# Two layers of conditioned attention: projections and turns moved behind the products on row tiles in each key tile

## The chip, the cores and the metric

One core of one Trainium2 chip. The metric is the device time of one execution in microseconds (us); lower is better. The kernel before takes 514.0 us, the median of 3 runs (513.84 to 514.3).

## What is computed

Two layers on x of 4 batches, 512 tokens, 256 channels, with 16 heads of width 16. Cut to what matters:

```python
# layer 0
xm  = rmsnorm(x) * (1 + scale) + shift            # scale, shift = cond @ w_cond
q, k, v = split(xm @ w_qkv); q, k = rope(q), rope(k)
x   = softmax(q @ k.T / 4) @ v @ w_out + x        # per head
# layer 1
xn  = layer_norm(x) * norm_w + norm_b
q, k, v = xn @ q_w + q_b, xn @ k_w + k_b, xn @ v_w + v_b
y   = softmax(q @ k.T + mask) @ v                 # per head
h   = layer_norm(y) * (1 + scale) + shift         # from silu(cond) @ emb_w + emb_b
x   = x + silu(h) @ out_w + out_b
```

## The kernel before

The work is cut into 32 groups: layer, batch, and 4 of the 16 heads. A group `s` has 4 key tiles `k` of 128 keys, so there are 128 key tiles, written (s, k) below. All engines walk the same hand-written order of steps (`order`, L206), which yields an opening and then `key_tile(s, k)` (L185) for every key tile; `KEY_TILE` (L43) is the order inside one.

The steps of a key tile, as TensorE runs them:

- `score` h and `shift` h (L510, L521), h from 0 to 3: the 128 x 512 scores of head h with keys on the partitions, then minus the maximum of each query added on top. Both contract over 64 rows. ScalarE then takes the exponential (L721).
- `max` h (`row_score`, L530): scores of head h of the group **two ahead**, queries on the partitions, 64 rows. VectorE reduces each to row maxima (L873, in layer 1 L870), the source of the later shifts.
- `half(h)` puts even heads on rows 0 to 63 of the array, odd heads on rows 64 to 127: these 12 products are on *row tiles*, and two neighbours of different halves run side by side.
- `values` (L547): probabilities of the key tile before, times values. Heads lie on four column tiles of 32.
- `maxima` (L555): the turn of the negated maxima of group s+1, in key tile 1 of each group. Behind it stand a copy by ScalarE and SyncE's DMAs of the shift.
- `output` (L562): the turn of the last group's output, in key tile 2 from group 1 on (31 in all); VectorE divides it by its sums (L895, L897).
- `pieces`: what `PIECES` deals out to single key tiles. `turn` (L582), `qk` (L593), `v` (L604), `y` (L621, the output projection, which VectorE adds to x), `embed` (L629, conditioning). They use the full array. `statistics` (VectorE only) stand just ahead of the pieces.

Every product into PSUM takes the next bank of a ring, in the order of the steps (`places`, L213). Ring A has 4 banks, is emptied by ScalarE in order and serves `score`, `maxima`, `qk`, `v`, and turns other than f1. Ring D has 3 banks, is emptied by VectorE in order and serves `max`, `output`, `y`, `embed` and turns f1. A product on ring D so waits until VectorE is done with the product three places before it (`d_free`, L501), one on ring A until ScalarE is done with the fourth before it (`a_free`). The rings follow `KEY_TILE`: move a step in it and its bank, its place in ScalarE's and VectorE's queue and the step it waits for all move with it.

GpSimd normalizes, splits and adds biases as its sources come; SyncE issues the DMAs of parts, operands, shifts and outputs in an order of its own.

Of the kernel before, what the change touches and what calls it, by code (L numbers as in the profile page):

```python
# [39 lines left out]

KEY_TILE = (("score", 1), ("score", 2), ("shift", 1), ("shift", 2), ("max", 1), ("pieces", None), ("output", None),  # L43
            ("max", 3), ("score", 0), ("score", 3), ("shift", 0), ("shift", 3), ("max", 0), ("maxima", None),
            ("values", None), ("max", 2))

RMS_W, NORM_W, NORM_B, Q_B, K_B, SBN_W, SBN_B, EMB_B, MASK = 0, 2, 4, 6, 8, 10, 12, 14, 18
# [137 lines left out]
def key_tile(s, k):  # L185

    for op, h in KEY_TILE:
        if op in ("score", "shift"):
# [24 lines left out]
def places():  # L213

    a, d = {}, {}
    for entry in order():
        op = entry[0]
        if op == "score":
            a[entry] = len(a)
        if op == "maxima":  # L220
            a["shift", entry[1]] = len(a)
        if op in ("max", "output"):
            d[entry] = len(d)
        if op == "piece":
            ring = d if entry[1][0] in ("y", "modulate", "embed") or entry[1][:2] == ("turn", "f1") else a
            ring[entry[1]] = len(ring)
    return a, d


A, D = places()  # L230
SCORED = [h for op, h in KEY_TILE if op == "shift"]
MAXED = [h for op, h in KEY_TILE if op == "max"]

# [1216 lines left out]
```

## Time and profile before

| | |
|---|---|
| median of 3 runs | 514.0 us |
| the profiled execution | 513.65 us |
| its span, first to last instruction | 511.9 us |
| TensorE busy | 501.6 us, 98% of the span |
| VectorE busy | 408.6 us, 80% |
| ScalarE busy | 345.7 us, 68% |
| GpSimd busy | 219.9 us, 43% |
| granted TensorE clock | 0.997 of full speed |

Busy shares are means over a span whose key tiles differ. The page adds up pipelined matmuls whose ends are modelled, so a busy TensorE may still be a waiting one: the starts of products in the timeline tell how long a key tile takes. "PEld" is the load of a weight into the array, "<-" in brackets names what ended an engine's idle time, and a row that ends in x6 stands for six instructions merged.

### The profile page before, as it was taken

What the parts mean: (1) busy time and instruction counts of PE and PEld (TensorE: products, weight loads), DVE (VectorE), ACT (ScalarE), POOL (GpSimd) and SP (SyncE); (2) the same over time, 40 slices, a digit from 0 to 9 for tenths busy, and PEclk for the clock granted to TensorE, in tenths of its full rate; (3) what the DMA queues carried; (4) which work ended last, traced back from release to release, by engine and by line L of the source; (5) the groups of instructions that cost most, each with busy time, mean ns of one, the idle gap of its engine ahead of it and who ended that gap; (6) DMA issues with size and microseconds to landing.
All of it is one profiled execution on the core that took longest, in us unless ns stands there. A gap on an engine that the chain in (4) does not pass through costs nothing.

```text
span 511.9 us, 9839 instructions
## 1 busy us (share of the span) xinstructions
PE 501.6 (98%) x3339; PEld 193.7 (38%) x3339; DVE 408.6 (80%) x1051; ACT 345.7 (68%) x679; POOL 219.9 (43%) x254
## 2 busy tenths in 40 slices
PE   9999899999999999999999999999999999999997
PEld 5553423333443244333443334332433333333234
DVE  4876897998897688966898678967899999999324
ACT  1552467776767675776768676777778778787863
POOL 3039749999143420832227430544573035005401
PEclk9999999999999999999999999999999999999999
DMA  6983232242214133110331123210431112211011
GB/s 243 351 273 101 75 103 75 66 143 82 77 53 125 41 125 121 46 43 8 119 125 44 42 90 114 68 33 32 125 124 44 43 43 85 81 46 44 2 41 42
DMA packets 43034, 45.26 MB, mean 88 GB/s; under 512 B 4436, under 2 KB 41572, under 8 KB 42600
## 3 DMA queue, kind: packets, MB, share of 16 engines
q1 hardware_dynamic: 42696, 42.79, 26.8%
q10 hardware_dynamic: 288, 1.84, 0.9%
q8 instruction: 27, 0.44, 0.3%
q14 instruction: 23, 0.19, 0.1%
HBM read 25.46 MB, written 18.87 MB: 87 GB/s over the span
## 4 chain that ended last, share of the span: by engine, by line
PE 74%; DVE 13%; issue 3%; ACT 2%; POOL 2%; DVEq 0%; ACTq 0%; POOLq 0%
PE bank L547 19%; PE bank L530 11%; PE bank L521 10%; PE bank L593 9%; PE bank L510 9%; DVE masked L870 8%; PE bank L621 5%; PE bank L604 5%; PE bank L562 2%; PE bank L582 2%; DVE row_max L873 1%; ACT probs L721 1%; PE bank L555 1%; PE bank L629 1%; POOL XN L844 1%
## 5 line engine op out<-in xcount | busy, mean ns | idle before, releaser
L721 ACT ACTIVATE probs<-bank 128x512 f32<-128x512 f32 x512 | 272.4, 601 | 82.0 <-PE bank L521 81.3
L873 DVE TENSOR_REDUCE row_max<-bank 128x1 f32<-128x512 f32 x256 | 163.0, 684 | 29.5 <-PE bank L530 27.8
L530 PE MATMUL bank<-k_s,q_s 64*128 64x512 f16 x512 | 183.0, 382 | 1.8 <-DVE row_max L873 1.2
L870 DVE CUSTOM_DVE_ANT_0 masked<-bank,mask_bias 128x512 bf16<-128x512 f32 x256 | 163.0, 687 | 13.0 <-PE bank L530 12.0
L510 PE MATMUL bank<-q_s,k_s 64*128 64x512 f16 x512 | 151.9, 381 | 0.9 <-ACT v_aug L789 0.5
L521 PE MATMUL bank<-shift,kx 64*128 64x512 f16 x512 | 148.8, 377 | 0.0
L547 PE MATMUL bank<-probs,v_aug 128*17 128x512 f32 x1024 | 135.4, 598 | 0.7 <-ACT probs L721 0.7
L530 PEld LDWEIGHTS bank<-k_s,q_s 64*128 64x128 f16 x512 | 46.3, 93 | 151.7 <-DVE row_max L870 67.1
L593 PE MATMUL bank<-xT,wqkv 128*128 128x512 f32 x128 | 61.8, 613 | 0.4 <-ACT xT L752 0.3
L521 PEld LDWEIGHTS bank<-shift,kx 64*128 64x128 f16 x512 | 46.9, 95 | 31.9
L510 PEld LDWEIGHTS bank<-q_s,k_s 64*128 64x128 f16 x512 | 31.7, 94 | 13.4 <-ACT probs L721 8.0
L593 PEld LDWEIGHTS bank<-xT,wqkv 128*128 128x128 f32 x128 | 22.2, 190 | 29.1 <-issue 24.9
L1123 POOL TENSOR_SCALAR spread<-moments_p 128x4 f32<-128x4 f32 x4 | 0.9, 228 | 72.5 <-DVE moments_p L908 72.5
L1135 POOL CAST parts<-plain 128x512 f16<-128x512 f32 x16 | 9.8, 610 | 51.7 <-ACT plain L770 51.7
L604 PE MATMUL bank<-wqkv,xT 128*128 128x256 f32 x128 | 31.3, 389 | 0.0
L547 PEld LDWEIGHTS bank<-probs,v_aug 128*17 128x17 f32 x1024 | 17.8, 95 | 33.1 <-issue 15.3
L1268 POOL TENSOR_SCALAR scaled<-row_max 128x16 f32<-128x16 f32 x10 | 2.6, 257 | 64.0 <-DVE row_max L870 39.9
L621 PE MATMUL bank<-wo,xT 128*128 128x256 f32 x112 | 27.9, 393 | 0.0
L604 PEld LDWEIGHTS bank<-wqkv,xT 128*128 128x128 f32 x128 | 23.3, 190 | 8.5 <-issue 4.1
L1170 POOL TENSOR_SCALAR v_bias<-vb_row,vecs 128x256 f32<-128x256 f32 x16 | 14.8, 926 | 23.2 <-ACT v_tmp L784 22.4
L919 DVE TENSOR_TENSOR X<-bank,X 128x512 f32<-128x512 f32 x14 | 9.6, 687 | 18.8 <-PE bank L621 18.8
L621 PEld LDWEIGHTS bank<-wo,xT 128*128 128x128 f32 x112 | 20.2, 190 | 8.1 <-DVE row_max L870 2.5
(112 smaller groups left out, 505.1 us busy)
## 6 DMA issues: line engine op xcount, KB each, us to landing
q_parts<-parts SPq DMA_DIRECT2D x64, 128.0 KB
k_parts<-parts SPq DMA_DIRECT2D x64, 128.0 KB
q_s<-q_parts SPq DMA_DIRECT2D x32, 256.0 KB, 2.8
k_s<-k_parts SPq DMA_DIRECT2D x32, 256.0 KB, 3.0
X<-in_x SPq DMA_DIRECT2D x4, 512.0 KB, 7.3
y<-X SPq DMA_DIRECT2D x7, 256.0 KB, 2.2
wc<-in_w_cond ACTq DMA_DIRECT2D x1, 1024.0 KB, 4.9
tables<-in_tables SPq DMA_DIRECT2D x4, 256.0 KB, 6.8
```

Of the source, the lines that this page charges most:

```text
L510: nc.tensor.matmul(bank, m.k_s[slot][rows, i, keys], m.q_s[slot][rows, i, :], start=True, stop=False)
L521: nc.tensor.matmul(a_bank(m, A["score", s, k, h]), keys, m.shift[s % SHIFTS][rows, i, :], start=False, stop=True).then_inc(q.a_made, 1)
L530: nc.tensor.matmul(bank, m.q_s[slot][rows, i, queries], m.k_s[slot][rows, i, :], start=True, stop=True).then_inc(q.d_made, 1)
L547: last = nc.tensor.matmul(m.ACC[W32 * h:W32 * h + W, :], m.v_aug[pu % VALUES][:, k, G * g + h, :], m.probs[k][:, h, :], start=(k == 0), st ...
L562: last = nc.tensor.transpose(bank[:, t * P:(t + 1) * P], m.oT[:, t * P:(t + 1) * P], m.ident[:, :])
L593: last = nc.tensor.matmul(bank, m.wqkv[layer][:, k, i * P:(i + 1) * P], m.xT[use % 2][:, k, :], start=(k == 0), stop=(k == CT - 1))
L604: last = nc.tensor.matmul(bank[:, t * C:(t + 1) * C], m.xT[use % 2][:, k, at], m.wqkv[layer][:, k, 2 * C:3 * C], start=(k == 0), stop=(k = ...
L621: last = nc.tensor.matmul(bank[:, t * C:(t + 1) * C], m.xT[use % 2][:, k, at], m.wo[layer][:, k, :], start=(k == 0), stop=(k == CT - 1))
L721: act.activation(m.probs[k][:, h, :], bank, ACT.Exp, scale=1.0 if s >= B * NG else float(DH) ** -0.5)\
L870: dve.tensor_tensor_reduce(m.masked[D["max", n, k, h] % ND][:, :], bank, m.mask_bias[:, b, :], 1.0, LOWEST, ALU.add, ALU.max, to)\
L873: dve.tensor_reduce(to, bank, AX.X, ALU.max).then_inc(q.d_done, 1)
L1170: pool.tensor_scalar(m.v_bias[:, :], m.vb_row[:, :], m.vecs[:, at:at + 1], None, ALU.mult)\
```

## The change

In `KEY_TILE` the entries `pieces` and `output` move from between `max 1` and `max 3` to between `max 0` and `maxima`. Nothing else differs; the work is the same.

```diff
-KEY_TILE = (("score", 1), ("score", 2), ("shift", 1), ("shift", 2), ("max", 1), ("pieces", None), ("output", None),
-            ("max", 3), ("score", 0), ("score", 3), ("shift", 0), ("shift", 3), ("max", 0), ("maxima", None),
+KEY_TILE = (("score", 1), ("score", 2), ("shift", 1), ("shift", 2), ("max", 1), ("max", 3), ("score", 0), ("score", 3),
+            ("shift", 0), ("shift", 3), ("max", 0), ("pieces", None), ("output", None), ("maxima", None),
             ("values", None), ("max", 2))
```

All engines follow, since they read the same order: ScalarE empties a piece of ring A behind the exponentials of heads 0 and 3 rather than ahead of them; VectorE takes statistics, residuals and outputs behind the maxima of heads 3 and 0; and both rings deal out their banks in the new order.

## Rows read from the trace of the kernel before

**Rows 1.** Page of the profile: busy time by engine, and shares of the last chain.

```profile
PE 501.6 (98%) x3339; PEld 193.7 (38%) x3339; DVE 408.6 (80%) x1051; ACT 345.7 (68%) x679; POOL 219.9 (43%) x254
...
PE 74%; DVE 13%; issue 3%; ACT 2%; POOL 2%; DVEq 0%; ACTq 0%; POOLq 0%
```

**Rows 2.** Timeline, key tile (10, 0): start us, us, engine, line, out<-in, count, [idle before].

```profile
203.17 0.39 PE L530 MATMUL bank<-k_s,q_s 64*128 64x512 f16 x1
...
203.92 2.00 PE L604 MATMUL bank<-wqkv,xT 128*128 128x256 f32 x8
...
204.62 0.68 DVE L873 TENSOR_REDUCE row_max<-bank 128x1 f32<-128x512 f32 x1
...
205.84 0.39 PE L530 MATMUL bank<-k_s,q_s 64*128 64x512 f16 x1
...
207.58 0.39 PE L530 MATMUL bank<-k_s,q_s 64*128 64x512 f16 x1
```

**Rows 3.** Timeline, key tile (10, 1), which no step cuts.

```profile
208.00 3.80 DVE L873 TENSOR_REDUCE row_max<-bank 128x1 f32<-128x512 f32 x6 [0.45 <-PE bank L530]
...
208.75 0.09 PEld L530 LDWEIGHTS bank<-k_s,q_s 64*128 64x128 f16 x1 [0.20 <-DVE row_max L873]
...
209.07 0.23 PE L555 MATMUL bank<-ident,neg_max 128*32 128x128 f16 x1
...
209.08 1.08 PE L547 MATMUL bank<-probs,v_aug 128*17 128x512 f32 x8
...
210.09 0.39 PE L530 MATMUL bank<-k_s,q_s 64*128 64x512 f16 x1
```

**Rows 4.** Timeline, key tile (10, 2), cut by the turn of an output.

```profile
210.84 0.66 PE L562 MATMUL bank<-ident,oT 128*128 128x128 f32 x4
...
211.43 0.39 PE L530 MATMUL bank<-k_s,q_s 64*128 64x512 f16 x1
...
213.17 0.39 PE L530 MATMUL bank<-k_s,q_s 64*128 64x512 f16 x1
```

**Rows 5.** Timeline of PE in the opening: token values, then the turn of maxima.

```profile
53.19 2.00 PE L604 MATMUL bank<-wqkv,xT 128*128 128x256 f32 x8
55.12 0.23 PE L555 MATMUL bank<-ident,neg_max 128*32 128x128 f16 x1
```

**Rows 6.** Timeline, key tile (0, 1), with two sets of row scores.

```profile
65.83 1.28 DVE L873 TENSOR_REDUCE row_max<-bank 128x1 f32<-128x512 f32 x2
...
69.69 0.39 PE L530 MATMUL bank<-k_s,q_s 64*128 64x512 f16 x1
```

**Rows 7.** Timeline, key tile (3, 0): a conditioning product and the first reduction behind negations.

```profile
102.24 0.39 PE L530 MATMUL bank<-k_s,q_s 64*128 64x512 f16 x1
...
103.83 0.68 DVE L873 TENSOR_REDUCE row_max<-bank 128x1 f32<-128x512 f32 x1
```

**Rows 8.** Timeline, key tile (4, 1): ScalarE behind a copy of token values.

```profile
119.23 0.39 PE L530 MATMUL bank<-k_s,q_s 64*128 64x512 f16 x1
...
119.43 0.60 ACT L789 ACTIVATE v_aug<-bank 128x512 f32<-128x512 f32 x1 [2.88 <-PE bank L547]
...
122.03 0.23 PE L555 MATMUL bank<-ident,neg_max 128*32 128x128 f16 x1 [0.37 <-ACT probs L721]
```

**Rows 9.** Timeline, key tile (21, 1): GpSimd's negated maxima and PE's turn of them.

```profile
371.16 0.22 POOL L1273 TENSOR_TENSOR neg_max<-scaled,neg_max 128x16 f16<-128x16 f32 x1
...
371.58 0.23 PE L555 MATMUL bank<-ident,neg_max 128*32 128x128 f16 x1
```

**Rows 10.** Timeline, key tile (22, 0): VectorE halves a turned tile of layer 1.

```profile
379.87 0.81 DVE L1005 TENSOR_SCALAR tables<-bank,mod 128x512 f32<-128x512 f32 x1
```

**Rows 11.** Timeline, key tile (25, 0): PE waits for a maximum behind statistics and residual.

```profile
416.74 0.09 PEld L530 LDWEIGHTS bank<-k_s,q_s 64*128 64x128 f16 x1 [0.28 <-DVE row_max L870]
```

**Rows 12.** Timeline, group 30: ScalarE's tanh and PE's wait behind it.

```profile
476.35 0.63 ACT L746 ACTIVATE tables<-tables 128x512 f32<-128x512 f32 x1 [0.55 <-DVE tables L1005]
...
478.98 0.09 PEld L555 LDWEIGHTS bank<-ident,neg_max 128*32 128x32 f16 x1 [0.82 <-ACT probs L721]
```


## The prediction, made before the changed kernel ran

> **What bounds the kernel now.** I read the page first: TensorE (PE below) is busy for 501.6 of 511.9 us and holds 74% of the last chain, VectorE 13% of it [rows 1]. So what moves PE's starts moves the end, and VectorE's share says where PE may be waiting behind a modelled end. Then I read the timeline of PE as starts of products, key tile by key tile, over the whole span. The 128 key tiles fall into few kinds. One with a lone piece on the full array lasts 4.41 us: 0.75 for three slots of products on row tiles, 1.92 for the piece, 1.74 for three more slots, the values (0.99) and the way back [rows 2]. One that nothing cuts lasts 2.51 us: 1.49 until the turn of the maxima, 1.02 from there to the next tile [rows 3]; without the maxima, whose turn and the values start 0.01 apart, it is 0.03 less. One cut by an output lasts 3.08, of which the output's turn takes 0.59 [rows 4].
>
> The reader is to see two things. First, a stretch of six slots is not two stretches of three without the seam. Its last product, max 0, needs the bank of max 2, the third before it on ring D. It starts at 208.75 (1.17 into the tile), and the idle row names the reduction [rows 3]. Six reductions fill 3.80 us there, so they start some 0.60 apart [rows 3]; two of them in 1.28 say the same [rows 6]. Four times that is 2.4: the uncut tile runs at VectorE's pace too, and a piece in the middle is what lets VectorE catch up. Second, pieces and outputs now follow max 0 at once, so on ring D their bank is that of max 1, whose reduction is young.
>
> **The change, part by part.** Times run from the tile's first product, max 2 of the tile before.
>
> *The seam.* Before: slots to 0.75, piece 1.92, then 1.74 [rows 2]. After: six slots until 1.49 [rows 3], piece 1.92, values and way back 0.99. That sums to 4.40 against 4.41. The saved seam pays for the wait of max 0 and no more. In parts: a slot lasts 0.22 (a six-slot stretch less a three-slot one is 0.74, less the wait of 0.08 at max 0, over three), so leaving three slots costs 0.75 - 0.66 = 0.09 more. One of two exits goes, one wait comes; read to the nanosecond that is 0.017 a tile.
>
> *Piece to values.* No trace of before shows the full array followed directly by values. Bounds: nothing, as between the turn of maxima and values (both on 32 columns, 0.01 apart [rows 3]), and 0.09, as between token values on the full array and the turn of maxima: 1.93 from start to start [rows 5], as much as the same block took to the row tiles behind it, 1.92 [rows 2], where the array changes its tiling for certain; the change is priced as the exit above. I take 0.09, which is already in the 1.92, since that row has the same two shapes of the array in the same order. A gain beyond nothing has no row.
>
> The Trainium skill (TensorEngine Tiling (Array Packing), Key Properties) says that a change of the tiling mode drains the engine. The row of 1.93 agrees [rows 5]. Counted by that rule alone, a lone piece passes three changes in place of four, which is the gain that rival A takes.
>
> *Pieces on ring A* (`qk`, `v`, turns p0, p1, f0; 35 tiles with such a piece). The bank is that of score 1. Its exponential is done by about 1.3, before the 1.49. So 35 x 0.017 = -0.6.
>
> *Outputs alone on ring D* (10 tiles: groups 4, 6, 10, 14, 18, 21, 24, 25, 28, 29). The first reduction starts at 0.42 (208.00 against 207.58 [rows 2, 3]), max 1's at 1.04, ends 0.69 later at 1.73 and frees PE at 1.77 to 1.79. The output wants the bank at 1.49 and waits some 0.28. The tile becomes 1.77 + 0.59 + 0.99 = 3.35 against 3.08 [rows 4]: +0.27 each, +2.7. Where a piece of ring A stands ahead of the output it covers the wait. Queued behind the waiting turn on PE are the values, max 2 and all of the next tile; VectorE and ScalarE then idle and give nothing back, as the next tile cannot go below its 2.47.
>
> *`y` on ring D* (12 tiles outside groups 30 and 31; in its own tile each). Same wait: 1.77 + 1.92 + 0.99 = 4.68 against 4.41, +0.27 each, +3.2. An output behind it is covered.
>
> *`embed` on ring D* (4 tiles). In (3, 0) VectorE negates maxima ahead of max 1's reduction, which starts 1.59 into the tile [rows 7] (1.45 in (10, 0) [rows 2]) and frees the bank at 2.33: 0.84 later than 1.49, of which that tile waits 0.14 already. +0.7 each in (2, 0) and (3, 0), +0.27 in the two with k=2: +1.9.
>
> *Turns f1 on ring D* (groups 22 and 26). The turn waits 0.3, and VectorE's halving of 0.81 [rows 10] already stretches these tiles by part of that: +0.4 a group, +0.8.
>
> *Key tile (0, 1)* has eight row scores. The reductions start at 65.83 and 66.43 [rows 6]; the next runs from 67.03 to 67.71. The last of the eight products needs it and starts at 67.77; qk ends its 1.92 at 70.0, the next tile starts at 71.0, against 69.69 [rows 6]. Before, the piece hid this. +1.3.
>
> *GpSimd* negates the maxima of group 22 only behind the biases of the token values of (20, 3), and PE's turn follows 0.20 after it [rows 9]. That piece ends 0.74 later (1.49 against 0.75), so the turn, which has nearly no slack, waits: +0.6, once. The other chains over GpSimd and SyncE (statistics to turned tiles, qk to parts, operands) start up to 1.3 later and have over 3 us of slack in the timeline. Taken at nothing; the normalized tiles wanted by the next p1 turn would be the first to be late.
>
> *What ScalarE gains.* Its queue is in order. In (4, 0) the copy of token values waits for the group's last values, with two exponentials behind it: it starts only at 119.43, and PE's turn of maxima comes 2.80 into (4, 1) rather than 1.49 [rows 8]. With the exponentials ahead of it, only the copies of values and output delay that tile; the turn comes near 1.82: -1.0. In group 30 ScalarE's tanh waits 0.55 for VectorE, the exponentials behind it, and PE waits for those [rows 12]. Behind them it blocks nothing, and 16 exponentials of 0.49 and the rest bind: -1.2. Tile (25, 0) waits 0.28 for a maximum behind statistics and a residual [rows 11]; taking the maxima first leaves 0.05: -0.5 for it and (29, 0). Lone pieces in group 31 lose a seam with no row scores to wait for: -0.2.
>
> **The sum.** +2.7 +3.2 +1.9 +0.8 +1.3 +0.6 = 10.5; -0.6 -1.0 -1.2 -0.5 -0.2 = -3.5; net +7.0. The profiled execution took 513.65, so 520.7; the median stands 0.35 higher, 514.0, and I predict 521.0.
>
> The same skill page (PSUM Bottleneck) warns that tiling speeds up TensorE but not the emptying of PSUM. The 0.28 at max 0 [rows 3] is of that kind.
>
> **The rivals.**
>
> *A, drains alone (faster).* If max 1's bank were free by 1.49 and max 2's by 1.09, no wait would come, and each of 72 tiles with a piece or output would save one exit of 0.094: -6.8, with ScalarE's gains 504. It decides on one number: the start of max 1's reduction, 0.8 and not 1.04. For it speaks that VectorE idles 0.45 us ahead of the first one; against it that the six reductions stand back to back behind that idle time [rows 3]. Chance 0.04.
>
> *B, piece to values for nothing (not slower).* The 0.094 goes in all 72 tiles, waiting ones too, as their wait lies ahead of the piece: 521.0 - 6.8 = 514.2. For it: values run on column tiles and start 0.01 behind the turn of maxima [rows 3]; against it the 1.93 [rows 5]. It decides at half of that price, 0.05, near 517.5. Chance 0.09.
>
> *C, the covers fall but ScalarE gives nothing back (slower).* If tile (4, 1) and group 30 keep their length because PE meets VectorE or the next bank there, the 2.7 us of relief and the half of (25, 0) don't come: 524. For it: GpSimd and VectorE stand in both chains [rows 8, 12]. Chance 0.09.
>
> **How the numbers follow.** Forecast 0.78, A 0.04, B 0.09, C 0.09. The range of the forecast alone is 519 to 522.5: the waits of ring D at 0.2 to 0.33 each, (0, 1) and GpSimd's wait between nothing and twice. With half of B and C it becomes 517.0 to 524.0. This kernel's runs tell some 0.2% from no change. Faster: A and a sliver of B, 0.05. Same (513 to 515): most of B, 0.07. Slower: 0.88.
>
> **What would show it.** Timeline: lone `qk` and `v` tiles keep 4.40, output tiles go from 3.08 to 3.35, `y` tiles from 4.41 to 4.68, with PE's weight load idle behind row_max at each first piece on ring D. From the last start of a piece to the values 0.31, not 0.22: if it is 0.22, B. (0, 1) ends 1.3 later, (4, 1) gets 1.0 and group 30 1.2 shorter. The forecast is wrong if the reductions start closer than 0.60, if pieces on ring A wait for exponentials, or if a late normalized tile adds waits at the p1 turns.

## The result, and the profile after

The changed kernel is slower: 524.6 us, the median of 4 runs (522.70 to 527.82), against 514.0; the ratio is 1.021, with a 95% interval of 1.018 to 1.024. The profiled execution took 522.70 us, its span 520.9, which is 9.0 us more than before. Its page has no row of the granted clock, and the lengths of its key tiles are those of full clock. Two things are thus to be explained: 9.0 us in that execution where I had worked out 7.0, and the 1.7 to 5.1 us more in the others.

From its page: busy time, and the chain that ended last.

```profile
PE 499.3 (96%) x3339; PEld 201.4 (39%) x3339; DVE 410.6 (79%) x1051; ACT 341.5 (66%) x679; POOL 219.9 (42%) x254
...
PE 66%; DVE 20%; issue 4%; ACT 2%; POOL 1%; DVEq 0%; ACTq 0%; POOLq 0%
```

PE's share of the chain fell from 74% to 66%, VectorE's rose from 13% to 20% [rows 1]: waits for maxima took the place of products. Split into key tiles by the starts of their products, the two traces differ as follows.

| key tiles | forecast, us | measured, us |
|---|---|---|
| 10 with an output alone | +2.7 | +2.7 (3.08 to 3.34, in layer 1 3.09 to 3.36) |
| 12 with `y` | +3.2 | +3.3 (without an output beside it 4.41 to 4.68 or 4.70) |
| 4 with `embed` | +1.9 | +2.3 |
| groups 22 and 26 | +0.8 | +0.9 |
| (0, 1) | +1.3 | +1.3 |
| (21, 1) | +0.6 | +0.8 |
| (7, 1), (11, 1), (15, 1), (19, 1) | 0 | +0.2 |
| the 32 other tiles with a piece of ring A | -0.6 | -0.5 |
| (4, 1) | -1.0 | -1.0 |
| (25, 0) and (29, 0) | -0.5 | -0.4 |
| group 30 | -1.2 | -0.5 |
| group 31 | -0.2 | -0.2 |
| sum, before rounding the parts | +7.0 | +9.0 |

The key tile cut by an output, in the trace after (start us, us, engine, line, out<-in, count, [idle before]); it answers to [rows 3, 4].

```profile
212.15 5.00 DVE L873 TENSOR_REDUCE row_max<-bank 128x1 f32<-128x512 f32 x8 [0.41 <-PE bank L530]
...
214.23 0.39 PE L530 MATMUL bank<-k_s,q_s 64*128 64x512 f16 x1
...
215.40 0.09 PEld L530 LDWEIGHTS bank<-k_s,q_s 64*128 64x128 f16 x1 [0.20 <-DVE row_max L873]
...
216.00 0.42 PEld L562 LDWEIGHTS bank<-ident,oT 128*128 128x128 f32 x4 [0.51 <-DVE row_max L873]
...
217.57 0.39 PE L530 MATMUL bank<-k_s,q_s 64*128 64x512 f16 x1
```

The turn stood at 0.75 into its tile; now it would be due at 1.49, some 215.72, and starts at 216.00, 1.77 into the tile. The row names the releaser: a reduction, in a row of eight that run 5.00 us with no gap over 0.03. It is the sixth of them, that of max 1: it starts 1.03 into the tile and ends at 1.71. The next tile starts 3.34 after this one, against 3.08.

A tile with `y` in the trace after:

```profile
142.69 0.39 PE L530 MATMUL bank<-k_s,q_s 64*128 64x512 f16 x1
...
143.86 0.39 PE L530 MATMUL bank<-k_s,q_s 64*128 64x512 f16 x1
144.46 1.59 PEld L621 LDWEIGHTS bank<-wo,xT 128*128 128x128 f32 x8 [0.50 <-DVE row_max L873]
...
146.38 0.13 PEld L547 LDWEIGHTS bank<-probs,v_aug 128*17 128x17 f32 x8 [0.33 <-issue]
...
147.37 0.39 PE L530 MATMUL bank<-k_s,q_s 64*128 64x512 f16 x1
```

The same 1.77 from tile to piece; then 1.92 for the piece and 0.99 for the values: 4.68.

A tile whose piece takes a bank of ring A, PE alone, which answers to [rows 2]:

```profile
207.32 0.39 PE L530 MATMUL bank<-k_s,q_s 64*128 64x512 f16 x1
...
208.50 0.39 PE L530 MATMUL bank<-k_s,q_s 64*128 64x512 f16 x1
208.81 1.99 PE L604 MATMUL bank<-wqkv,xT 128*128 128x256 f32 x8
210.74 1.05 PE L547 MATMUL bank<-probs,v_aug 128*17 128x512 f32 x8
211.72 0.39 PE L530 MATMUL bank<-k_s,q_s 64*128 64x512 f16 x1
```

From token values to values it takes 1.93, what [rows 5] had to the turn of maxima: the change of tiling between the full array and column tiles costs what an exit from row tiles does. The whole tile takes 4.40 against 4.41. The saved seam and the wait at max 0 (208.50, 1.18 into the tile) cancel, as forecast. From the last start of a product of the piece to the values it is 0.31, the number that the prediction named against rival B.

### The profile page after: what moved, and what is told of

It reads as the page before. It is cut to its first block, busy times and chain, and to the rows that moved or that the text cites. A ratio compares the mean times of both kernels' runs of the same rounds, so it can differ in the third digit from the quotient of the medians.

```text
span 520.9 us, 9839 instructions
## 1 busy us (share of the span) xinstructions
PE 499.3 (96%) x3339; PEld 201.4 (39%) x3339; DVE 410.6 (79%) x1051; ACT 341.5 (66%) x679; POOL 219.9 (42%) x254
## 4 chain that ended last, share of the span: by engine, by line
PE 66%; DVE 20%; issue 4%; ACT 2%; POOL 1%; DVEq 0%; ACTq 0%; POOLq 0%
PE bank L547 18%; DVE masked L870 12%; PE bank L593 9%; PE bank L521 8%; PE bank L530 8%; DVE row_max L873 6%; PE bank L510 6%; PE bank L621 5%; PE bank L604 4%; PE bank L562 3%; PE bank L582 3%; PE bank L629 1%; ACT probs L721 1%; POOL XN L844 1%; DVE row_max L870 1%
## 5 line engine op out<-in xcount | busy, mean ns | idle before, releaser
L721 ACT ACTIVATE probs<-bank 128x512 f32<-128x512 f32 x512 | 264.4, 605 | 97.3 <-PE bank L521 97.1
L873 DVE TENSOR_REDUCE row_max<-bank 128x1 f32<-128x512 f32 x256 | 160.1, 684 | 37.5 <-PE bank L530 37.1
L870 DVE CUSTOM_DVE_ANT_0 masked<-bank,mask_bias 128x512 bf16<-128x512 f32 x256 | 161.3, 687 | 18.9 <-PE bank L530 18.3
L530 PE MATMUL bank<-k_s,q_s 64*128 64x512 f16 x512 | 171.8, 381 | 2.5 <-DVE row_max L873 2.3
L510 PEld LDWEIGHTS bank<-q_s,k_s 64*128 64x128 f16 x512 | 37.0, 94 | 17.8 <-ACT probs L721 5.1
L728 ACT ACTIVATE oT<-bank 128x512 f32<-128x512 f32 x31 | 18.6, 601 | 6.8 <-PE bank L547 6.6
```

The source lines that it names most:

```text
L510: nc.tensor.matmul(bank, m.k_s[slot][rows, i, keys], m.q_s[slot][rows, i, :], start=True, stop=False)
L530: nc.tensor.matmul(bank, m.q_s[slot][rows, i, queries], m.k_s[slot][rows, i, :], start=True, stop=True).then_inc(q.d_made, 1)
L721: act.activation(m.probs[k][:, h, :], bank, ACT.Exp, scale=1.0 if s >= B * NG else float(DH) ** -0.5)\
L728: act.activation(m.oT[:, :], m.ACC, ACT.Copy).then_inc(q.acc_copied, 1)
L870: dve.tensor_tensor_reduce(m.masked[D["max", n, k, h] % ND][:, :], bank, m.mask_bias[:, b, :], 1.0, LOWEST, ALU.add, ALU.max, to)\
L873: dve.tensor_reduce(to, bank, AX.X, ALU.max).then_inc(q.d_done, 1)
```

## The experiments

Each of these kernels is the kernel before or the changed kernel with a small edit. Where an edit says which tiles are moved, `key_tile` yields statistics, pieces and output either behind max 1 (as before) or behind max 0 (as changed), by a condition:

```diff
+    place = "behind" if CONDITION else "middle"
...
+        if op == place:
+            # statistics, pieces, and the output where k == 2
```

All times are medians; the kernel before took 513.98, 514.15 and 514.26 us beside them.

**The changed kernel again** (no edit), for the spread of its executions.

> The changed kernel itself, once more, beside the others. Its profiled execution took 522.7 us, its other executions 524.4 to 527.8, at a granted clock of 0.99 where the profiled one shows 1.0. Theory 1 (TensorE's waits of the changed order let its clock fall in some executions): here again some executions above 524 us, each with a clock below 0.995 and some 1.7 to 5 us more than one at 1.0. Theory 2 (the higher times were a chance of that chip): all executions within 0.3% of 522.7 us, whatever the clock.

It took 524.34 us (522.95 to 527.53, 4 runs). Over both sets the executions at a mean clock of 1.0 took 522.70 and 522.95; one at 0.993 took 524.79; those at 0.990 took 523.99, 524.44, 524.7 and 527.82; one at 0.987 took 527.53. This time the profile fell on that last one. Its page gives the granted clock in 40 slices:

```profile
PEclk8899999889999999999999999999999999999999
```

Busy times and clock of four stretches of that trace: a stretch in (2, 0), one close behind it, one in (3, 0), and one in (3, 1).

```profile
core 0: us, PE busy (x) PEld busy (x) DVE busy (x) ACT busy (x) POOL busy (x), PEclk, DMA share, GB/s
91.42:94.40 2.98, 1.89 (x20) 0.95 (x16) 2.91 (x6) 2.30 (x5) 2.76 (x4) 1.00 0.00 0
95.10:98.50 3.40, 3.40 (x18) 0.65 (x20) 1.08 (x4) 1.21 (x3) 3.23 (x3) 0.50 0.00 0
106.83:111.50 4.67, 2.75 (x28) 1.69 (x28) 4.58 (x8) 2.30 (x5) 4.36 (x5) 1.00 0.50 140
112.25:115.60 3.35, 3.35 (x21) 0.98 (x21) 2.51 (x4) 2.67 (x6) 3.10 (x4) 0.50 0.00 0
```

In (2, 0) and (3, 0), waits included, PE is busy for 1.89 of 2.98 us and 2.75 of 4.67 us; behind each, once the four-column products have run, the granted clock is 0.50, its 1.2 GHz level. PE's rows in (3, 0) and behind it:

```profile
110.31 1.03 PE L629 MATMUL bank<-es,wc 128*128 128x4 f32 x8 [1.92 <-DVE row_max L873]
...
112.25 1.03 PE L510 MATMUL bank<-q_s,k_s 64*128 64x512 f16 x2
112.66 1.05 PE L521 MATMUL bank<-shift,kx 64*128 64x512 f16 x2
```

PE idles 1.92 us ahead of products of four columns, and then a slot takes 0.42 in place of 0.22: (3, 1) lasts 4.01 us where it lasted 2.51. Tile by tile, this execution is longer than the other profiled one by 0.8 in (2, 0), 0.7 in (2, 1) and 1.5 in (3, 1), all at 1.2 GHz; by 0.9 in (3, 0) at full clock, where VectorE's two negations take 1.55 us and PE's wait grows; by 0.3 in (27, 0); and by 0.65 in the opening. So 3.0 of its 4.8 us are lost in key tiles at the lower clock. A mean clock alone does not tell where the clock fell: executions of the kernel before have a mean of 0.993 too, and in its profile the lower clock stands in the opening. Theory 1 holds as far as an observation goes; its cause is tested below.

**Ring A behind, ring D ahead.** CONDITION: the first piece of the tile takes a bank of ring A.

> Half of the change: only in key tiles whose first moved step takes a bank of ring A (qk, v, turns p0, p1, f0) do pieces and output stand behind max 0; where ring D comes first (y, embed, turns f1, an output alone) they stay behind max 1. Theory 1 (ring D's waits are the loss): lone qk and v tiles 0.017 shorter each (-0.6 us), tile (4, 1) -1.0, key tile (0, 1) +1.3, (21, 1) +0.8, (7, 1) and its like +0.06 each: net +0.8, so 514.8 us and the profiled span about 512.7. Theory 2 (any step between the stretch and the values costs, by a change of tiling or a colder order): each of 35 tiles some 0.1 longer, 518 us or more.

It took 516.15 us (514.70 to 516.63), ratio 1.003 (1.002 to 1.004). At a clock of 1.0 an execution took 514.70, the 514.8 of theory 1, and no lone `qk` or `v` tile grew. The rest is the clock at (0, 1), which the profile caught:

```profile
core 0: us, PE busy (x) PEld busy (x) DVE busy (x) ACT busy (x) POOL busy (x), PEclk, DMA share, GB/s
60.00:64.40 4.40, 3.41 (x18) 0.85 (x16) 3.14 (x7) 2.22 (x5) 1.84 (x3) 1.00 0.74 206
64.41:72.93 8.52, 7.54 (x29) 2.23 (x30) 5.67 (x11) 3.45 (x8) 5.52 (x5) 0.80 0.02 5
72.93:90.00 17.07, 16.93 (x118) 5.52 (x114) 14.00 (x25) 12.15 (x24) 9.45 (x9) 1.00 0.40 121
```

That tile lasts 8.52 us at a mean clock of 0.80, where the changed kernel's profile has 7.26. In this case no four-column product is near: ahead of the fall PE waits 0.21, 0.21 and 0.63 us for maxima between its row scores. So theory 1's account of places is right, and it lacked the clock.

**Ring D behind, ring A ahead**, the other half. CONDITION: the first step to move takes a bank of ring D.

> The other half: only where ring D's bank comes first (y, embed, turns f1, outputs alone) are pieces and output moved behind max 0. Theory 1 (ring D's waits): +0.27 in each lone output and y tile (+6.0), embed +0.75, +0.91, +0.33, +0.32 (+2.3), turns f1 +0.9, less 0.4 in (25, 0) and (29, 0), 0.5 in group 30 and 0.2 in group 31: +8.1, so 522.1 us at full clock. Theory 2: 518 or less.

It took 523.34 us (521.94 to 524.53), ratio 1.018. The executions near full clock, 521.94 and 522.29, meet the 522.1 of theory 1; the others are those at 0.99. All outputs and `y` grew by 0.27, and (0, 1) was 5.94 again. So the greater part of the loss lies in this half; (0, 1) and (21, 1) are in the other.

**Reductions of half the length.** In both kernels VectorE's maximum, in layer 1 the fused mask and maximum too, reads only the first 256 of 512 keys, and the exponential's scale is a quarter of what it should be, so that it stays finite with such maxima. Nothing else is left out. The line of layer 0:

```diff
-            dve.tensor_reduce(to, bank, AX.X, ALU.max).then_inc(q.d_done, 1)
+            dve.tensor_reduce(to, bank[:, 0:256], AX.X, ALU.max).then_inc(q.d_done, 1)
```

> The kernel before, with VectorE's reductions over 256 of the 512 keys (so its maxima are those of half the keys, and the exponential's scale is a quarter, to stay finite). It shortens what frees ring D from 0.69 to about 0.42 us. Expected: uncut tiles lose the wait of 0.08 at max 0, some 55 x 0.08 = 4.4 us, so about 509 us. Both theories say so; it is the base of the next kernel.

> The changed kernel with the same shortened reductions. Theory 1 (the loss is ring D waiting for reductions; without it each seam is worth one exit of 0.094): lone qk and v tiles 4.31 against 4.41, 72 x 0.094 = 6.8 us and ScalarE's 1.7 us gained, 0.8 lost at (21, 1): 7 to 8 us less than the kernel before with short reductions, about 501.5. Theory 2 (the loss lies in what stands between the stretch and the values, in changes of tiling or weights): as slow as that kernel or slower, 509 to 518.

The first took 506.02 us (505.38 to 506.48), 3 us less than I gave it: the uncut tiles lost their 0.09, as said, but the tiles from (0, 0) to (0, 2), where VectorE is the slower engine, lost 2.1 and (25, 0) and (29, 0) 0.9. The second took 500.52 (500.32 to 503.93): 5.5 us **less** than its base, where the same change had cost 10.6 (in the profiled executions 0.5 of it is (19, 0), which lasted 4.12 us in the base and 3.58 in the kernel before). The reduction in that trace, and one lone-piece tile of each kernel, first the order of before, then the changed one:

```profile
L873 DVE TENSOR_REDUCE row_max<-bank 128x1 f32<-128x256 f32 x256 | 95.9, 418 | 79.0 <-PE bank L530 77.3
```

```profile
199.59 0.39 PE L530 MATMUL bank<-k_s,q_s 64*128 64x512 f16 x1
...
200.34 1.99 PE L604 MATMUL bank<-wqkv,xT 128*128 128x256 f32 x8
202.27 0.39 PE L530 MATMUL bank<-k_s,q_s 64*128 64x512 f16 x1
...
204.00 0.39 PE L530 MATMUL bank<-k_s,q_s 64*128 64x512 f16 x1
```

```profile
198.03 0.39 PE L530 MATMUL bank<-k_s,q_s 64*128 64x512 f16 x1
...
199.43 1.99 PE L604 MATMUL bank<-wqkv,xT 128*128 128x256 f32 x8
201.35 1.05 PE L547 MATMUL bank<-probs,v_aug 128*17 128x512 f32 x8
202.34 0.39 PE L530 MATMUL bank<-k_s,q_s 64*128 64x512 f16 x1
```

With 0.42 us reductions six slots end at 1.40, the piece starts at once, and the tile takes 4.31 against 4.41. 60 of the key tiles got 0.10 or 0.11 shorter, outputs and `y` among them, about what an exit from row tiles costs (0.094). That is rival A's world, and it shows that ring D's wait for reductions, not the order of shapes on the array, makes the change slow. I had expected 7 to 8 us of gain: (2, 0), (3, 0), (21, 1), (0, 1) and (27, 0) still lost 3.0 between them, and (7, 1) and its like 0.16 each.

**Conditioning products ahead.** CONDITION: not (2, 0), (2, 2), (3, 0), (3, 2).

> The changed kernel, with the pieces and outputs of the four key tiles with a conditioning product (2, 0), (2, 2), (3, 0), (3, 2) back behind max 1. Theory 1 (the low clock comes from those tiles' waits and four-column products): at full clock 2.3 us less than the 522.7 of the changed kernel, 520.4; no stretch at the lower clock from 85 to 120 us of the span, and a spread below 1.5 us, what is left of it coming from key tile (0, 1). Theory 2 (the clock falls for another reason): executions still spread over 4 to 5 us.

It took 521.07 us (520.61 to 523.05). The four tiles have the lengths of before again (-2.3), and the profile shows no lower clock anywhere in its span, (0, 1) included. The executions at full clock, 520.61 and 521.0, stand 0.2 to 0.6 over the forecast; in 521.0, the profiled one, 0.5 of it is a late load of keys in (27, 0). The spread is smaller than the changed kernel's but not below 1.5 us: one execution took 523.05, at 0.997 and with no profile, and stays unexplained.

**Idle products in the waits.** The changed kernel, with PE kept busy ahead of the conditioning products.

```diff
                 pe.wait_ge(q.es_step, 3)
+                group, k = 2 + piece[1] // 2, 2 * (piece[1] % 2)
+                keep_busy(1 if k else 4, a_free(A["score", group, k + 1, 1]))
```

> The changed kernel, with idle products of 512 columns (four in (2, 0) and (3, 0), one in (2, 2) and (3, 2)) on PE in the wait ahead of each conditioning product, into the bank of ring A that the next score takes. They add work, no row of a result, and end before the awaited maximum. Theory 1 (PE's idle wait lets the clock fall): no lower clock around those tiles, 522.5 to 523.5 us in nearly all executions, 1 to 2 us less than the changed kernel's median of 524.4. Theory 2: 524.5 or more, with the same spread.

It took 523.84 us (523.03 to 524.72), half a microsecond less than the changed kernel, which the changed kernel's own spread does not tell from nothing; two of the four lie outside the 522.5 to 523.5 of theory 1. From 92.8 to 120 us the clock is 1.00, though each tile still waits as long; but the profile has the dip at (0, 1), and that tile lasts 8.93. Half of theory 1's claim stood, so the next kernel fills both places.

```diff
         if op == "max":
+            fill = {(2, 1, 3): 4, (2, 1, 0): 2}.get(tuple(at), 0)
+            if fill:
+                keep_busy(fill, a_free(A["qk", 0, 3, 1]))
             row_score(*at)
```

> The changed kernel with idle products in the waits ahead of the conditioning products, as before, and in key tile (0, 1) too: four ahead of row score 3 and two ahead of row score 0 of the second group, into the bank that qk takes next. Theory 1 (PE's idle waits let the clock fall): (0, 1) stays at its 7.3 us of full clock, no lower clock behind the opening, and all executions within 1 us of 522.8. Theory 2 (the fall has another cause): the lower clock at (0, 1) or later comes back in some executions, with 524 us and more.

It took 523.65 us, and all four executions lie between 523.44 and 523.79. The spread of 5 us is gone. The changed kernel was not run again beside it, so this compares sets that were taken apart. Windows of its trace: ahead of (0, 1), (0, 1) and its surroundings, and the tiles of the conditioning products.

```profile
core 0: us, PE busy (x) PEld busy (x) DVE busy (x) ACT busy (x) POOL busy (x), PEclk, DMA share, GB/s
60.00:64.40 4.40, 3.41 (x21) 0.93 (x20) 3.41 (x6) 2.50 (x5) 1.62 (x2) 1.00 0.64 176
64.40:72.60 8.20, 7.85 (x41) 2.30 (x37) 5.83 (x12) 3.18 (x7) 5.53 (x5) 1.00 0.05 15
90.00:120.00 30.00, 29.88 (x236) 11.97 (x232) 25.87 (x49) 19.83 (x41) 28.04 (x26) 1.00 0.31 91
```

The clock is 1.00 in all three. The idle products themselves held (0, 1) up by 0.37 us, which I had not forecast, and a late normalized tile cost (15, 0) 0.66 in that execution. In the profile with the first fills alone the filled tiles kept their clock and the unfilled (0, 1) lost it; here (0, 1) kept it too. More work on PE in the same waits takes the dips away, so PE's idle stretches are their cause as far as two profiles and eight times can show. The gain is small: 0.7 to 1.0 us off the changed kernel's two medians, 0.4 us of idle products in (0, 1) already paid.

**The six tiles of the long waits ahead.** CONDITION: not (0, 1), (2, 0), (2, 2), (3, 0), (3, 2), (20, 3).

> The changed kernel with the six key tiles of the long waits put back behind max 1: (0, 1), the four with a conditioning product, and (20, 3), on whose token values GpSimd's negation of (21, 1) waits. Theory 1: 522.7 less 1.3, 2.3 and 0.8 is 518.3 us, with no lower clock behind the opening, so all executions within 0.8 us. What is left over the kernel before, 4.3 us, is then the waits of 0.27 in 22 tiles and of 0.4 in groups 22 and 26, less ScalarE's gains. Theory 2 (clock falls for another reason): a spread of 4 us as in the changed kernel.

It took 518.83 us (518.49 to 518.96), ratio 1.009 (1.008 to 1.010), and its five executions lie within 0.5 us. So 0.5 over the forecast; of the profiled execution's excess 0.26 is again in (27, 0) and 0.3 in the opening. This is the second test of the waits: taken away rather than filled, they leave no wide spread either. What remains of the loss is the 0.27 of outputs and `y` and groups 22 and 26.

**Behind max 0 only where it pays.** CONDITION: the group is 30 or 31, or ring A comes first and the tile is none of (0, 1), (7, 1), (11, 1), (15, 1), (19, 1), (20, 3).

> Pieces and output behind max 0 only where the trace says that it pays: first ring A, but not in (0, 1), (7, 1), (11, 1), (15, 1), (19, 1) and (20, 3), and in all tiles of groups 30 and 31, which have no row scores. Theory 1: -0.5 us from 29 seams, -1.0 in (4, 1), -0.5 in group 30, -0.2 in group 31: 511.9 us against 514.0, ratio 0.996. Theory 2 (these gains are given back elsewhere, the last chain being VectorE's): 514 us.

It took 512.31 us (511.93 to 512.55), ratio 0.9966 with an interval of 0.9954 to 0.9979: faster than both kernels, by 1.7 us where 2.2 were worked out. In the profiled execution the key tiles give 2.0, and the opening, which the edit leaves alone, is 0.6 longer than in the profile of before. Of the 2.0, 1.0 comes from key tile (4, 1):

```profile
120.07 0.60 ACT L795 ACTIVATE v_aug<-bank 128x512 f32<-128x512 f32 x1 [1.88 <-PE bank L553]
...
121.04 2.07 ACT L727 ACTIVATE probs<-bank 128x512 f32<-128x512 f32 x4
...
121.70 0.23 PE L561 MATMUL bank<-ident,neg_max 128*32 128x128 f16 x1 [0.26 <-ACT probs L727]
```

The copy of token values now has no exponential of its own tile behind it, and PE's turn of maxima starts 1.82 into the tile, not 2.80 [rows 8]. Groups 30 and 31 give 0.7 and the seams some 0.4; a tenth is lost again in (2, 0) and other tiles.

## Why the prediction was right or wrong

The direction was right, and so was the mechanism that makes up most of the loss, ring D's wait for young reductions. The time, 524.6, lay 0.6 us above the range and 3.6 above the forecast of 521.0. Two things failed. The steps took each new wait of PE at its length and put nothing for the clock, which in most executions fell behind such waits; and terms of the sum were off by 2.0 us together, `embed` by 0.4 and group 30 by 0.7 above all. The other 1.6 us of the median are the clock and small differences between executions. Either miss alone would have left the time inside the range. By steps:

- *The seam*: right. 4.40 against 4.41, with the wait at max 0 paying back what the saved exit gave; the short reductions gave the exit alone as 0.10. There are 36 such tiles beside (0, 1), not 35, and the 0.28 that a sentence behind the sum gives for the wait at max 0 is that of the outputs; at max 0 it is 0.08.
- *Piece to values*: right. 1.93, as the row of the opening had it, so rival B is out.
- *Outputs and `y` on ring D*: right to 0.1 us over 22 tiles. The wait is 0.28, from max 1's reduction. (The six reductions in 3.80 us of [rows 3] stand 0.62 apart in the mean, not 0.60; the step's 1.04 held all the same: in the cut tile max 1's starts 0.61 behind the first one.)
- *(0, 1)*: right. Its last product, qk and next tile came where the steps put them:

```profile
67.77 0.39 PE L530 MATMUL bank<-k_s,q_s 64*128 64x512 f16 x1 [0.21 <-DVE row_max L873]
68.08 1.98 PE L593 MATMUL bank<-xT,wqkv 128*128 128x512 f32 x4
70.00 0.23 PE L555 MATMUL bank<-ident,neg_max 128*32 128x128 f16 x1
...
71.02 0.39 PE L530 MATMUL bank<-k_s,q_s 64*128 64x512 f16 x1
```

- *`embed`*: 2.3 in place of 1.9. In (3, 0) the conditioning product started 2.58 into the tile, not 2.33. Of that, 0.17 is VectorE's first negation, which took 0.48 us, not the 0.30 of before. The rest is in all four tiles: from the end of the reduction to the first weight load it takes 0.12 us, where an output or `y` takes 0.05, and why stays open. GpSimd's row stands beside the negation:

```profile
105.08 1.16 POOL L1157 TENSOR_TENSOR parts<-roped,parts 128x512 f16<-128x512 f32 x1
...
105.78 0.48 DVE L881 TENSOR_SCALAR neg_max<-row_max 128x16 f16<-128x16 f32 x1
...
107.22 0.91 PE L629 MATMUL bank<-es,wc 128*128 128x4 f32 x7 [1.03 <-DVE row_max L873]
```

GpSimd's instruction ends at 106.24, the negation at 106.26. It is no chance: 5 of 44 negations (L881, L883) were stretched over 0.2 us in the profile of before and 11 of 44 in that of after, and all 16 end 0.03 us behind the end of a GpSimd instruction in which they started. (In each trace one negation that began in the same 0.01 us as GpSimd's instruction kept its 0.17 us.) So the step took a duration from one execution that depends on what GpSimd runs beside it, and in the changed order more negations start while GpSimd has long to go. The Trainium skill (SBUF — State Buffer, SBUF: two separate sides) has the pair of SBUF ports that the two engines share as a lock held for a whole instruction; these rows agree, and no run here takes GpSimd's work away to prove it.

- *GpSimd at (21, 1)*: 0.8 in place of 0.6, by the step named; PE's turn waits for its negation, as before [rows 9], only longer:

```profile
377.86 0.22 POOL L1273 TENSOR_TENSOR neg_max<-scaled,neg_max 128x16 f16<-128x16 f32 x1
...
378.22 0.22 PE L555 MATMUL bank<-ident,neg_max 128*32 128x128 f16 x1 [0.63 <-POOL neg_max L1273]
```

- *Pieces of ring A wait for nothing*: wrong in four tiles. In (7, 1) and its like ScalarE has two turned tiles and the output's copy ahead of score 1's exponential, and `qk` starts 1.57 into the tile (which began at 163.59), not 1.49. The step left out ScalarE's backlog from the tile before, though the prediction had named such a wait as a sign of being wrong.

```profile
165.16 0.30 PEld L593 LDWEIGHTS bank<-xT,wqkv 128*128 128x128 f32 x2 [0.31 <-ACT probs L721]
```

- *Group 30*: wrong in size, -0.5 for -1.2. I let ScalarE's work fill the time without gaps. Its tanh now stands at the end of the tile's queue, waits for VectorE's halving all the same, and holds up the output's copy and the first exponential of the next tile:

```profile
486.51 0.63 ACT L746 ACTIVATE tables<-tables 128x512 f32<-128x512 f32 x1
...
487.52 2.05 ACT L721 ACTIVATE probs<-bank 128x512 f32<-128x512 f32 x4
```

The block moved by one tile, it did not go.

- *The clock*: the step that was missing. I looked for who waits and for how long, tile by tile, and took each wait at its length. In (2, 0) and (3, 0) a long wait stands beside products of four columns, in (0, 1) several shorter ones stand close together, and the profiles have the clock at 1.2 GHz behind one or the other. Six of the changed kernel's eight executions took 523.99 us or more at a mean clock of 0.993 or less. The median stands 1.9 us over the profiled execution at full clock; how much of that is the clock no profile says, since only one execution with dips was profiled, and there it was 3.0 of 4.8. The two fills show the cause; which execution gets a dip stays open.

Rival A fell on the number that it named: max 1's reduction starts 1.03 into the tile, and only with shorter reductions does its gain come. Rival C fell for (4, 1), where ScalarE gave back the full 1.0, and half held in group 30.

## What to carry to other kernels

Where a hand-written order feeds a ring of few banks, price a moved step by the reduction that frees its new bank, not only by the seams that the move saves: here 0.09 us saved a tile stood against 0.08 at one bank and 0.28 at another. Decide tile by tile which side of the cut a piece belongs on, by the ring that it uses and by what stands ahead of it in each engine's queue; the part of this change that pays was worth 0.3%, and the whole cost 2%. And look where new idle stretches of TensorE fall close together: there they can cost the clock as well.

## What the runs showed of the hardware that was not expected

Idle stretches of TensorE of 1.1 and 1.9 us beside four-column products (in the second set of the changed kernel), and of 0.2, 0.2 and 0.6 us close together without such products (with ring A behind), were followed by 1.2 GHz; in other executions of the same orders they were not, and the changed kernel's times spread over 5 us. Idle products in the same waits brought four executions within 0.35 us. VectorE's negation of 128 x 16 maxima took from 0.17 to 1.20 us for operands of the same shape, and in the two traces compared each of the 16 over 0.2 us ended 0.03 us behind an instruction of GpSimd.
